# A two-layer graph network on one core: another order of the opening, and preparatory work moved into block 0 of the first layer

## The reference, cut to what matters

```
# x (2048, 256), adj (2048, 2048) of 0/1 int32
h = max(layernorm(x), 0)
# layer 0
deg = sum(adj > 0, axis=1);  agg = (adj > 0) @ h / max(deg, 1)
x = x + relu(concat(h @ W_self + b_self, agg @ W_nb + b_nb) @ W_comb + b_comb)
# layer 1, on h2 = max(layernorm(x), 0): five steps of a gated graph network
for _ in range(5):
    a = concat(adj @ (s @ in_W.T + in_b), adj.T @ (s @ out_W.T + out_b), s)
    r, z = sigmoid(a @ r_W.T + r_b), sigmoid(a @ z_W.T + z_b)
    s = (1 - z) * s + z * tanh(concat(a[:, :512], r * s) @ h_W.T + h_b)
x = x + tanh(s @ o1_W.T + o1_b) @ o2_W.T + o2_b
```

## Time and profile before

| | us |
|---|---|
| median of three executions | 1374.04 |
| span of the profiled execution, first to last instruction | 1372.5 |
| PE busy | 1354.4 (99%) |
| DVE busy | 464.9 (34%) |
| ACT busy | 224.5 (16%) |
| first product of the layer-0 loop starts at | 40.31 |
| last product of block 0 of layer 0 starts at | 58.12 |

### The profile page before, as it was taken

How to read it: one execution, slowest core, us unless ns; L and a number is a source line. 1 busy time by engine, 2 the same in 40 slices (tenths; PEclk the granted TensorE clock), 3 DMA queues, 4 the chain that set the end, 5 groups by cost and what they waited for, 6 DMA issues and landing times.

```text
span 1372.5 us, 14932 instructions
## 1 busy us (share of the span) xinstructions
PE 1354.4 (99%) x5322; PEld 654.9 (48%) x5322; DVE 464.9 (34%) x882; ACT 224.5 (16%) x439; POOL 3.0 (0%) x9
## 2 busy tenths in 40 slices
PE   7999999999999999999999999999999999999998
PEld 5666544444444444444444444444444444444445
DVE  6577732314142230423224032322413323141225
ACT  4756110101121010111101011110101101010011
POOL 0000000000000000000000000000000000000000
PEclk9999999999999999999999999999999999999999
DMA  8454200000000000000000000000000000000021
GB/s 280 154 169 139 85 0 0 0 0 1 0 1 0 0 0 0 0 0 0 0 0 0 0 0 0 0 0 0 0 0 0 0 0 0 0 0 0 0 80 62
DMA packets 16796, 33.40 MB, mean 24 GB/s; under 512 B 1025, under 2 KB 6402, under 8 KB 16386
## 3 DMA queue, kind: packets, MB, share of 16 engines
q1 hardware_dynamic: 15760, 29.23, 6.5%
q0 software_dynamic: 720, 3.67, 0.7%
q10 hardware_dynamic: 290, 0.14, 0.0%
HBM read 27.27 MB, written 5.77 MB: 24 GB/s over the span
## 4 chain that ended last, share of the span: by engine, by line
PE 90%; DVE 0%; issue 0%; ACT 0%; DVEq 0%
PE bank L205 88%; PE bank L398 1%; PE bank L321 0%; DVE H L738 0%; PE bank L274 0%; DVE DR L706 0%; DVE AT L695 0%; DVE A L877 0%; DVE stat L645 0%; PE bank L294 0%; ACT H L493 0%; DVE nrm L672 0%; DVE nrm L671 0%; DVE nrm L670 0%; DVE nrm L669 0%
## 5 line engine op out<-in xcount | busy, mean ns | idle before, releaser
L205 PE MATMUL bank<-work,WG 128*128 128x512 f32 x1120 | 485.9, 592 | 0.0
L205 PE MATMUL bank<-AT,SN 128*128 (+1 forms) x1280 | 485.1, 379 | 0.0
L205 PE MATMUL bank<-A,SN 128*128 (+1 forms) x1280 | 485.1, 379 | 0.0
L205 PEld LDWEIGHTS bank<-work,WG 128*128 128x128 f32 x1120 | 211.9, 190 | 262.1 <-issue 262.1
L833 DVE SCALAR_TENSOR_TENSOR work<-DR,gcol,bank 128x512 f32<-128x512 f16 x120 | 89.7, 748 | 394.4 <-PE bank L205 394.0
L205 PEld LDWEIGHTS bank<-A,SN 128*128 (+1 forms) x1280 | 125.2, 98 | 154.3 <-issue 6.3
L205 PEld LDWEIGHTS bank<-AT,SN 128*128 (+1 forms) x1280 | 125.2, 98 | 152.3 <-issue 4.5
L610 ACT ACTIVATE work<-work,col 128x512 f32<-128x512 f32 x120 | 86.6, 722 | 549.1 <-DVE work L837 549.1
L808 DVE TENSOR_SCALAR work<-bank 128x512 f32<-128x512 f32 x40 | 25.8, 686 | 385.8 <-PE bank L205 385.8
L205 PE MATMUL bank<-ST,WG 128*128 128x512 f32 x320 | 140.6, 592 | 0.0
L205 PEld LDWEIGHTS bank<-ST,WG 128*128 128x128 f32 x320 | 60.8, 190 | 69.8 <-issue 67.0
(11 more groups left out here) (80 smaller groups left out, 489.8 us busy)
## 6 DMA issues: line engine op xcount, KB each, us to landing
WG<-in_adj SPq DMA_DIRECT2D x32, 512.0 KB, 4.7
SN<-in_x SPq DMA_DIRECT2D x2, 1024.0 KB, 10.7
x_d<-SN POOLq DMA_DIRECT2D x4, 512.0 KB, 2.9
A<-x_d SPq DMA_DIRECT2D x1, 2048.0 KB, 8.2
out<-A SPq DMA_DIRECT2D x4, 512.0 KB, 2.9
A<-in_wg_t SPq DMA_DIRECT2D x2, 768.0 KB, 6.2
fused_d<-AT POOLq DMA_DIRECT2D x1, 1536.0 KB, 6.4
WG<-fused_d SPq DMA_DIRECT2D x1, 1536.0 KB, 6.9
```

The source lines that it names most:

```text
L205: return pe.matmul(o, l, r, start=start, stop=stop)
```

## The change

SP issues half of the gate weights, then both halves of x, then the other half; w0 and w_comb come after the first three adjacency chunks. On PE only the fused products and the 24 products for gcol stay in the opening. `turn_h(0..3)` move into the loop, behind `mean_sum` of pairs 6, 8, 10 and 12 and into banks 6 and 7 alone; W12 and bias0 (`combine`) move behind `mean_sum(14)`. ACT copies gcol ahead of its first conversions, and its high part of h is now a Relu of h32, of quarter 0 in the opening and of quarters 1 to 3 at i = 2, 5 and 8. DVE no longer takes the maximum over h32: h32 holds the unclipped h times 2048, and the low part, the high part and the copies of the transposed h clip it. `normal(0)`, `normal(1)`, `low(0)` stay in the opening; the rest is at i = 2, 5 and 8 in the loop. `mean_sum` waits for one quarter of h at a time.

```diff
+HIGH_AT = [2, 5, 8]
+TURN_AT = [6, 8, 10, 12]
+COMBINE_AT = 14
@@ sync
-            for w, w_half in enumerate((w_in, w_out)):
+            weights(0, w_in)
             for h in range(2):
                 sp.dma_start(xs[:, 8 * h:8 * h + 8, :], x_v[:, 8 * h:8 * h + 8, :]).then_inc(ld_x[h], 16)
-            sp.dma_start(w0R, ...); sp.dma_start(wcR, ...)
+            weights(1, w_out)
             for k in range(2 * 4 * NB):
+                if k == RING:
+                    sp.dma_start(w0R, ...); sp.dma_start(wcR, ...)
@@ tensor, after the fused products
+            (24 products for gcol).then_inc(gcol_sum, 1)
+            def combine():
+                pe.wait_ge(ld_w0, 32); pe.wait_ge(hT_act, 2); pe.wait_ge(hT_dve, 2)
+                (8 products for W12 into bank[6], bank[7]).then_inc(w12_sum, 1)
+                pe.wait_ge(left_ready, 1)
+                pe.wait_ge(w12_out, 2)
+                (5 products for bias0 into bank[6]).then_inc(setup_done, 1)
@@ mean_sum(i)
-                if m == 0 and b == 0:
-                    pe.wait_ge(h_hi, 4); pe.wait_ge(h_lo, 4); pe.wait_ge(w12_out, 1)
+                if m % BT == 0 and b == 0:
+                    pe.wait_ge(h_hi, m // BT + 1)
+                    pe.wait_ge(h_lo, m // BT + 1)
@@ tensor, the loop
                 mean_sum(i)
+                if i in TURN_AT:
+                    turn_h(TURN_AT.index(i))
+                if i == COMBINE_AT:
+                    combine()
@@ scalar
+            act.wait_ge(gcol_sum, 1)
+            copy(gcol, bank[3]).then_inc(w12_out, 1)
             for k in range(2):
                 for r in range(2):
                     convert(k, r)
+            high(0)
@@ scalar, the loop, after convert and move_adj(i)
+                if i in HIGH_AT:
+                    high(HIGH_AT.index(i) + 1)
+                if i - 1 in TURN_AT:
+                    move_h(TURN_AT.index(i - 1))
+                if i - 1 == COMBINE_AT:
+                    combined()
@@ vector
-            newton(NT, 1)
+            rs = newton(NT, 1)
+            link(v.tensor_scalar(rs, rs, SCALE, None, ALU.mult))
-                v.tensor_scalar(hq, hq, 0.0, None, ALU.max).then_inc(h_ready, 1)
+            normal(0); normal(1); low(0)
@@ vector, the loop
+                if i in HIGH_AT:
+                    low(HIGH_AT.index(i) + 1)
+                if i in HIGH_AT[:2]:
+                    normal(HIGH_AT.index(i) + 2)
                 if i:
                     make_mask(i - 1)
+                if i - 1 in TURN_AT:
+                    turned_h(TURN_AT.index(i - 1))
                 if i % NT == 0 and i:
                     sums(i // NT - 1)
                 if i % 2 == 1:
                     move_adj(i)
```

More of the change, by code:

```diff
@@ L159, in _, with weights @@
             x_v = x.rearrange("(t p) d -> p t d", p=P)
-            for w, w_half in enumerate((w_in, w_out)):
+            def weights(w, w_half):
                 sp.dma_start(ioR[:, w], w_half.rearrange("(j p) f -> p j f", p=P)).then_inc(ld_w[w], 16)
@@ L221, in turn_h @@
                 pe.wait_ge(h_ready, b + 1)
-                if b < 2:
-                    pe.wait_ge(fused_out, 2 * b + 6)
-                else:
-                    pe.wait_ge(hT_act, b - 1)
-                    pe.wait_ge(hT_dve, b - 1)
+                if b == 0:
+                    pe.wait_ge(fused_out, 8)
+                else:
+                    pe.wait_ge(hT_act, b)
+                    pe.wait_ge(hT_dve, b)
                 for f in range(FT):
                     for q in range(BT):
-                        last = pe.transpose(bank[4 + 2 * (b % 2) + f][:, q * P:q * P + P],
+                        last = pe.transpose(bank[6 + f][:, q * P:q * P + P],
                                             h32[:, BT * b + q, f * P:f * P + P], ident)
@@ L233, in _ @@
             pe.wait_ge(ld_c, 48)
[L235 to L247, removed]
             for w in range(2):
@@ L253, in _ @@
                                   col[:, 2 * w + j:2 * w + j + 1], j == 0, j == 1)
-            last.then_inc(setup_done, 1)
-            turn_h(2)
-            turn_h(3)
+            last.then_inc(gcol_sum, 1)
+            def combine():
+                pe.wait_ge(ld_w0, 32)
+                pe.wait_ge(hT_act, 2)
+                pe.wait_ge(hT_dve, 2)
+                for w in range(2):
+                    for i in range(2):
+                        for j in range(2):
+                            last = mm(bank[6 + w][:, i * D:i * D + D], w0R[:, j, w * D + i * P:w * D + i * P + P],
+                                      wcR[:, 2 * w + j, :], j == 0, j == 1)
+                last.then_inc(w12_sum, 1)
+                pe.wait_ge(left_ready, 1)
+                pe.wait_ge(w12_out, 2)
+                for j in range(4):
+                    mm(bank[6][:, 0:D], L0[:, j, :], wcR[:, j, :], j == 0, False)
+                mm(bank[6][:, 0:D], cst[0:1, C_ONE:C_ONE + P], raw["b_comb"][0:1, :], False, True).then_inc(setup_done, 1)
             def turn_adj(i):
@@ L301, in dense @@
                 pe.wait_ge(agg_dve, b + 1)
+                if b == 0:
+                    pe.wait_ge(w12_out, 3)
+                    pe.wait_ge(hT_act, NB)
+                    pe.wait_ge(hT_dve, NB)
                 if b > 0:
@@ L529, in _ @@
             nc.scalar.activation(nrm[:, 1, :], nrm[:, 0, :], ACT.Sqrt).then_inc(sqrt_ready, 1)
+            act.wait_ge(gcol_sum, 1)
+            copy(gcol[:, :, :].rearrange("p w t -> p (w t)"), bank[3][:, 0:12]).then_inc(w12_out, 1)
             for k in range(2):
@@ L532, in _, with high, combined @@
                     convert(k, r)
-            for q in range(4):
+            def high(q):
                 act.wait_ge(h_ready, q + 1)
-                copy(hi_lo[:, BT * q:BT * q + BT, 0, :], h32[:, BT * q:BT * q + BT, :], SCALE).then_inc(h_hi, 1)
+                nc.scalar.activation(hi_lo[:, BT * q:BT * q + BT, 0, :], h32[:, BT * q:BT * q + BT, :],
+                                     ACT.Relu).then_inc(h_hi, 1)
             def move_h(q):
                 act.wait_ge(hT_ready, q + 1)
[L538 to L548, removed]
+                nc.scalar.activation(ST[:, 0, q * BN:q * BN + BN], bank[6][:, :], ACT.Relu,
+                                     scale=1.0 / SCALE).then_inc(hT_act, 1)
+            def combined():
+                act.wait_ge(w12_sum, 1)
+                for w in range(2):
+                    ins = copy(W12[:, 2 * w:2 * w + 2, :].rearrange("p k n -> p (k n)"), bank[6 + w][:, :])
+                ins.then_inc(w12_out, 1)
+                act.wait_ge(setup_done, 1)
+                copy(bias0, bank[6][:, 0:D]).then_inc(w12_out, 1)
+            high(0)
             def block_end(b):
@@ L672, in newton, with normal @@
                 link(v.reciprocal(rs, sc))
-            newton(NT, 1)
-            for q in range(4):
+                return rs
+            rs = newton(NT, 1)
+            link(v.tensor_scalar(rs, rs, SCALE, None, ALU.mult))
+            def normal(q):
                 for t in range(BT * q, BT * q + BT):
@@ L678, in _, with low, turned_h @@
                                           ALU.subtract, ALU.mult)
-                link(ins)
-                hq = h32[:, BT * q:BT * q + BT, :].rearrange("p t d -> p (t d)")
-                v.tensor_scalar(hq, hq, 0.0, None, ALU.max).then_inc(h_ready, 1)
-            for q in range(4):
+                ins.then_inc(h_ready, 1)
+            def low(q):
                 dve.wait_ge(h_hi, q + 1)
                 v.scalar_tensor_tensor(out=hi_lo[:, BT * q:BT * q + BT, 1, :], in0=h32[:, BT * q:BT * q + BT, :],
-                                       scalar=SCALE, in1=hi_lo[:, BT * q:BT * q + BT, 0, :],
-                                       op0=ALU.mult, op1=ALU.subtract).then_inc(h_lo, 1)
+                                       scalar=0.0, in1=hi_lo[:, BT * q:BT * q + BT, 0, :],
+                                       op0=ALU.max, op1=ALU.subtract).then_inc(h_lo, 1)
+            def turned_h(q):
                 dve.wait_ge(hT_ready, q + 1)
-                v.tensor_copy(ST[:, 1, q * BN:q * BN + BN], bank[5 + 2 * (q % 2)][:, :]).then_inc(hT_dve, 1)
+                v.tensor_scalar(ST[:, 1, q * BN:q * BN + BN], bank[7][:, :], 0.0, 1.0 / SCALE,
+                                ALU.max, ALU.mult).then_inc(hT_dve, 1)
+            normal(0)
+            normal(1)
+            low(0)
             def move_adj(i):
```

11 lines of the change are left out of this document (4 added, 7 removed).

## The result

The changed kernel is slower: 1395.32 us (1394.55 to 1396.20, four runs) against 1374.20 for the kernel before on the same chip; ratio 1.0153, 95% interval 1.0138 to 1.0167. The profiled execution took 1396.2 with a span of 1394.4, so 1.8 us lie around the span. Its last product of block 0 starts at 80.42 us, 22.3 later than before; the span is 21.9 longer. So all of the loss lies ahead of that product. This execution was the longest of the four; by the medians the loss is 21.1 us.

What follows compares the result with a forecast made beforehand. PE was taken to bound the kernel, with no slack behind block 0. Moved work and hand-overs put its last product 21.3 us later, half clock 1.2 more: 1374.0 + 22.5 = 1396.5 us, range 1386 to 1411.

Steps and rivals of the forecast that it cites:

- rival A: Block 0: in-order engines hand over at each moved piece and PE waits; +19 to +27 us, chance 0.62; the forecast itself.
- The opening: Up to the first product: square root ends at 22.4, gcol at 27.6, first product at 32.95 us, 7.35 earlier than before.
- Pairs 1 and 4: Pieces ahead of their masks use up the lead: 7.35 to 2.9 us at pair 1, 0.4 behind at pair 4.
- adjacency chunk 3: Ahead of pair 1: its slot is free at 29.0 and it lands at 33.4 us at the earliest, holding ACT's conversion.
- The half clock at pair 1: PE stands from 33.9 to 38.65 us, so pair 1 runs at half clock and later work comes 1.2 us later.
- Pairs 7 to 13: PE waits 4.6 us ahead of pair 7 and 1.8 ahead of 9, 11, 13; 5.95, then 14.5 us behind.
- The clock's fall behind the pause of pair 7: Rival B: pauses from pair 7 on make the clock fall repeatedly, some 3 us each; +27 to +40 us, chance 0.22.
- My sign for that rival: In the profile after, a PE clock below 1.00 between 50 and 80 us would speak for the clock rival, chance 0.22.
- Combine: Behind pair 14: W12 3.45, wait for ACT's copies 1.15, bias0 2.15; 6.75 us added.
- rival C: Block 0 and opening: shorter hand-overs than in the timetable, or an earlier first product; +3 to +19 us, chance 0.12.
- all stalls hidden, still 2.7 behind: Lower bound for block 0: PE's own work alone puts the last product at 60.8 us, 2.7 behind.
- Rival D: Opening and block 0: gcol ends earlier and every stall is hidden; 1.0 us faster, 1373.0, chance 0.04.

Runs made afterwards that it cites:

- experiment 5: Kernel before with only both halves of x loaded ahead of the second half of the gate weights; 1376.01 us, ratio 1.0012.
- experiment 7: experiment 3 with ACT copying gcol behind its first four conversions and the high part of quarter 0; 1377.28 us, ratio 1.0017 to the kernel before.
- experiment 1: Changed kernel with ACT's and DVE's copies of the transposed h one pair later; 1387.58 us, ratio 1.0086 to the kernel before.
- experiment 2: Changed kernel with DVE's low part and normalisation in the loop behind mask and move_adj; 1385.97 us, ratio 1.0076 to the kernel before.
- experiment 3: Changed kernel with the edits of experiment 1 and experiment 2 together (both orders mended); 1380.65 us, ratio 1.0039 to the kernel before.
- experiment 4: Changed kernel with 22 needless 384-column products on PE in the pause ahead of pair 7; 1393.56 us, ratio 1.0132 to the kernel before.
- experiment 6: Changed kernel with W12 and bias0 back in the opening ahead of gcol, their loads ahead of the adjacency; 1396.09 us, ratio 1.0154 to the kernel before.
- experiment 8: Packed version: loads as before, W12 and bias0 behind fused, gcol in two groups of twelve, transposes of h in the loop, orders mended; 1373.42 us, ratio 0.9997.
- experiment 11: experiment 8 with all 24 gcol products in one stretch behind fused, ahead of W12 and bias0; 1374.61 us, ratio 1.0001 to the kernel before.
- experiment 9: experiment 8 with gcol in six groups of four, ahead of pair 0 and behind pairs 0 to 4; median 1380.73 us, ratio 1.0030 to the kernel before.
- experiment 10: experiment 8 with two gcol products behind each of pairs 1 to 12, turn_h(0) in the opening; median 1372.56 us, ratio 0.9995 to the kernel before.

## Why the prediction was right

It said 1396.5, and 22.5 us more at the last product of block 0; measured were 1395.32 and 22.3. Its rival A, hand-overs of in-order engines, is what happened. Point by point, starts in us:

| pair | before | predicted | after |
|---|---|---|---|
| 0 | 40.31 | 32.95 | 32.69 |
| 1 | 41.5 | 38.65 | 37.86 |
| 4 | 45.05 | 46.65 | 45.38 |
| 7 | 48.6 | 55.75 | 54.08 |
| 9 | 51.0 | 60.95 | 60.62 |
| 15 | 58.12 | 80.6 | 80.42 |

(Predicted from pair 4 on with the 1.2 us of the clock in it.)

*The opening.* Right to 0.3 us: the square root ended at 22.70 for 22.4 in spite of statistics at 16.5, and gcol at 27.5 for 27.6. Run by itself, the order of loads puts the first product 1.2 us later (experiment 5). Which wait held the first product, gcol ahead of the conversions, was shown by experiment 7. That gcol took 6.93 us for 7.1 is in part luck: with the same opening it took 5.9 to 7.6 in experiments 1 to 4.

*Pairs 1 and 4.* Pair 1 started 0.8 us earlier than predicted. I had the adjacency chunk 3 land at 33.4 at the earliest; ACT converted it at 32.82 without a wait. The sum itself had slipped: 29.0 and 3.9 make 32.9, not 33.4. I also had PE stand still from 33.9 on; at half clock the work behind pair 0 lasted until 35.1, so the pause was 2.75 us, not 4.75. The half clock at pair 1 came as forecast (pair 1 took 2.22 us instead of 1.19, pair 2 1.79). It put the transposes behind pair 1, and with them `high(2)` and mask 4, about 1.0 us later, where I had added 1.2. So pair 4 was 1.3 us early, of which 0.8 came from pair 1.

*Pairs 7 to 13.* PE's pauses were 4.06, 1.50, 1.50 and 1.50 us. From the end of the transposes, as I had counted, they are 4.28 and 1.73, for 4.6 and 1.8 predicted: behind the transposes PE also does `turn_adj`, 0.2 us. That 0.2 is already in the 1.19 us of a pair, so the timetable counted it twice at pairs 9, 11 and 13. Undoing each order alone took away the pauses that belong to it and left the others (experiments 1 and 2; only that ahead of pair 4 was 1.40 in experiment 1, where the clock was half for longer), so the cause is shown, not only argued.

*What I had wrong in size.* The clock's fall behind the pause of pair 7 was a rival with a chance of 0.22, to be repeated and to cost 3 us a time. It happened once and cost 1.6 (experiment 4); the forecast had put it at nothing. My sign for that rival, a clock below 1.00 between 50 and 80 us, did appear, and stood for 1.6 of its 18 us. Combine took 7.5 us instead of 6.75: W12 3.7, its wait 1.3 and bias0 2.5. The fall and the longer combine made up for a start of pair 7 that was 1.7 us early and for the 0.2 us counted twice. So the agreement to 0.2 us at pair 15 is partly luck; each term is right to about 1.6 us. The range was also described more kindly than it was: 1386 is +12, so it held 12 to 19 of rival C's +3 to +19, which is the smaller part.

*The account of the whole.* The first product starts 7.6 us earlier; block 0, first to last product, is 47.7 instead of 17.8 us. Of these 29.9 us 13.5 are waits for masks and 1.3 the wait in combine; the remaining 15.1 are PE work: transposes 4.3, combine 6.2, and about 4.6 us for half clock, of which about 1 only takes the place of waiting ahead of pair 1. The bound "all stalls hidden, still 2.7 behind" had the right sign: with both orders mended the kernel was still 5 us slower than before (experiment 3). Rival D, that the mended version gains, needed gcol out of the way as well, and even then it was 2 us behind (experiment 7).

The rule of the Trainium skill that I weighed against the change ("TensorE: Matmul & The Clock Gate", the section on the clock gate), idle time brings the clock down and busy time brings it back, is borne out by the 4.06 us pause, behind which the clock fell and, with the pause filled, did not (experiment 4), by the fall inside the same pause in experiment 6, and by its return at 41.3 and 58.4 us with PE at work. But experiment 8 shows a fall without idle time: PE was busy without a pause from 17.8 us on, and the clock fell at 29.8. The Trainium skill's rule that relu stands in every table set ("ScalarE: Activation LUTs", the section on table sets) agrees: no table load appears between the square root at 22.48 and the end of block 0, and Relu took 1.05 us, as the copy had.

## What to carry to other kernels

Moving preparatory work under a loop is no gain if the loop's bound engine has to do it: here PE was full in block 0, and the opening's stall was worth less than the work. If such work is moved anyway, put each copy and each wait behind the operation that the next product needs, not ahead of it; an iteration or two of difference on an in-order engine was worth 9 to 11 us here (the ratios of experiments 1 and 2 against 1.0153). And before a load is moved ahead, follow what its consumer waits for next: the statistics came 3 us earlier and the square root 2 us later.

## What the runs showed of the hardware that I had not expected

- Back-to-back one-column products, each with a full weight load, did not keep the clock up, though PE read 100% busy. Each longer stretch of them was followed by half clock: begun at 27.3 us, the clock fell at 30.8 in the kernel before; 20.6 and 24.2 in the changed kernel; 26.5 and 29.8, then 32.9 and 36.4 in experiment 8; 19.3 and 21.9 in experiment 11. With 0.9 us of them (1.85 at half clock) in each pair the clock stayed at half for 24 us with PE never pausing (experiment 9).
- The same order of instructions ran in 1371 or in 1381 us, by whether the clock fell (experiment 9; experiment 10 with 1372 or 1380): the mean granted clock of the short executions is 0.999 to 1.000, of the long ones 0.991 to 0.994. What decides it in an execution is not shown. A median over few runs can hide this; the list of all runs shows it.
- Where the clock falls beside a pause differs. In the changed kernel it did not fall in the pause of 4.06 us ahead of pair 7, but about 1 us after work had begun again. In experiment 6 the same pause, again 4.06 us, saw it fall inside, at 59.2 us with PE idle since 56.8, and pairs 7 and 8 ran at half from their start. A pause filled with needless products was faster than an empty one by 1.6 us (traces of experiment 4 and of the changed kernel).

```profile
59.00:60.00 1.00, 0.00 (x0) 0.00 (x0) 0.59 (x1) 0.98 (x3) 0.00 (x0) 0.60 0.00 0
```
